# The last 512 tokens of the merge stage go as two chunks of 256 tokens, the very last chunk in two halves of 128

## The chip, the core and the metric

The kernel runs on one core of a Trainium2 chip. The metric is the device time of one execution, in microseconds (us). Three executions of the kernel before took 2415.31, 2416.16 and 2416.76 us, so its median is 2416.16 us. Engines are written as in the profile: PE is TensorE, DVE is VectorE, ACT is ScalarE, POOL is GpSimd, SP is SyncE. PE's clock has two levels, 1.2 and 2.4 GHz; the profile gives the granted clock as a share of the higher one.

## What is computed

The input x has 8 x 1024 tokens of 256 numbers. The reference, cut to what the change touches:

```python
# first half: attention and a memory MLP on the normalised tokens, merged by two gates
out_swa = _swa(x_in, wq, wk, wv, wo)
...                                   # gradients of the MLP give updated weights upd
out_mem = _mlp(*upd, k_flat)          # silu(x @ w1.T + b1) @ w2.T + b2, hidden size 1024
g1 = sigmoid(out_swa @ lin1.T)
g2 = sigmoid(out_mem @ lin2.T)
x = x + (g1 * out_swa + g2 * out_mem)
# second half: 8 experts, the top 2 of each token
h = _layernorm(x)
probs = softmax(h @ gate_w.T + gate_b)
topk_prob, topk_idx = top_k(probs, 2)
...                                   # slot of a token = its rank among the tokens of its expert
y = relu(rows @ W1[e] + b1) @ W2[e] + b2
x = x + probability * y
```

## The kernel before

The kernel has four phases, each a block of five engine programs that ends with all engines meeting: attention, gradient, merge and experts. The change is in the merge phase (about 1410 to 1945 us of the span).

**Chunks.** The merge phase takes the 8192 tokens in chunks. `SIZES` gives the blocks of 128 tokens in each; before, it is 16 chunks of 4 blocks (512 tokens), C = 0 to 15. `parts_of(C)` gives the parts in which the end of a chunk's work is done: one part of all four blocks, except for the last chunk, which has two parts of two blocks.

**Work of a chunk.** For chunk C, in fp32r products that are each split into three matmuls (`matmul_split`, L105):
- `hidden(C, t)`, t = 0 to 7: 6 matmuls each into one of three PSUM banks `ps_z`; ACT makes the sigmoid (`m_sig`, L1980), DVE multiplies (`m_hf`, L2121), ACT rounds the high half (`m_hh`, L1985), POOL subtracts to get the low half (`m_hl`, L2369; for t = 7 DVE does it, L2126). `hidden(C, t)` waits until DVE has read the bank of t - 3.
- `gate1(C)`: 12 matmuls; `memory_out(C, m, half)`: 4 times 12 matmuls, which wait for the low halves; `gate2(C)`: 12 matmuls.
- `second_term` and `merge` on DVE (L2136 and L2147), `residual`: 2 transposes for each block on PE (L1897) and an add on DVE (L2183), then the layernorm: `norm_stats` (L2191 to L2200) on DVE, the root on POOL (`root`, L2375), `norm_apply` (L2208) on DVE, transposes of the result on PE (`transpose_x2`, L1906), copy by ACT (`copy_x2T`, L2038), the router's matmuls (`router`, L1916), then on DVE the top two experts (`router`, `shift`, `choose_experts`, L2223 to L2262), exp on ACT (L2051, with a table load before it and one after it, when the next sigmoid comes), and `dispatch`: small matmuls on PE (L1928) and ten small operations on DVE (L2273 to L2292). At last POOL scatters the rows to their expert slots with indirect DMAs (L844), one for each block and each of the two choices k.

**Order.** Each engine runs a list written out by hand. In the loop's turn for chunk C the work of three chunks is interleaved: the matrix products of C, the end of C - 1 (gate2, merge, residual, norm, router) and the dispatch and scatter of C - 2. On DVE the turn is: hidden 0 and 1, `second_term(C - 1)`, hidden 2, `merge(C - 1)`, hidden 3, `weigh(C - 2)`, hidden 4, `choose_experts(C - 2)`, hidden 5 to 7, `residual(C - 1)`, the low half of hidden 7, `dispatch(C - 2)`, `norm_stats` and `norm_apply(C - 1)`, then the splits for the next chunk and the router of C - 1. On PE `transpose_x2(C - 1)` stands before the last 12 matmuls of `memory_out`, and `router(C - 1)` ends the turn. On ACT the turn ends with `copy_x2T(C - 1)`, `split_x2(C - 1)`, `memory_out(C, 1)` and `exponent(C - 1)`. In the last chunk's turn ACT and DVE also split the first expert's W1 (L2089 and L2341).

**After the loop** the last chunk's own end is done with nothing of a later chunk beside it. PE's list there:

```python
            gate2_part(NCH - 1, 0)
            dispatch(NCH - 2)
            gate2_part(NCH - 1, 1)
            keep_busy(2)
            residual(NCH - 1, 0)
            keep_busy(2)
            residual(NCH - 1, 1)
            keep_busy(12)
            ...                       # transpose_x2 and router of both parts
            keep_busy(4)
            dispatch(NCH - 1)
            keep_busy(32)
```

`keep_busy(n)` is n matmuls of 512 columns (L1956) whose results nobody reads. POOL does, after the loop, the roots of the last chunk's parts and the k = 0 scatters of the last two chunks. The k = 1 scatters of the last two chunks stand at the start of the expert phase on POOL, ahead of the gathers of its first round. The expert phase starts when all engines have ended the merge phase; SP then loads the first expert's rows once the k = 0 scatters have landed.

Of the kernel before, what the change touches and what calls it, by code (L numbers as in the profile page):

```python
# [14 lines left out]
P = 128  # L15
# [21 lines left out]
T = GRP * P  # L37
SIZES = [GRP] * (NBLK // GRP)
NCH = len(SIZES)
# [857 lines left out]
def parts_of(C):  # L897

    return [slice(0, 2), slice(2, 4)] if C == NCH - 1 else [slice(0, GRP)]

# [803 lines left out]
def merge_phase(nc, io, sems, shared, routed, halves, g1, g2, b1n, b2n, chunk_in, first_w1, first_w2):  # L1704
    with ExitStack() as ctx:
# [120 lines left out]
        def part_bank(n):  # L1826

            return ps_z[n]
# [8 lines left out]
        def tensor(e):  # L1837
# [29 lines left out]
            def gate2_part(C, n):  # L1867
                (wh, wl), cols = lin[1], columns(parts_of(C)[n])
                acc = part_bank(n)[:].rearrange("p (m t) -> p m t", m=KC)
                pe.wait_ge(*om_low.at(C, 1))  # L1870
                pe.wait_ge(*h_made.at(C, HC - 1))
                for m in range(KC):
                    mc = slice(m * P, (m + 1) * P)
                    i = matmul_split(e, acc[:, m], [(wh[:, k, mc], wl[:, k, mc]) for k in range(KC)],
                                     [(omh[:, k, cols], oml[:, k, cols]) for k in range(KC)])
                i.then_inc(*gate2_done(C, n))
# [13 lines left out]
            def residual(C, n):  # L1890
                blocks = parts_of(C)[n]
                pe.wait_ge(*merged.at(C, n))
                pe.wait_ge(*ident_in.at(0))
                pe.wait_ge(*x2T_full.at(*final_part(C - 1)))
                for j in range(blocks.start, blocks.stop):
                    for m in range(KC):
                        i = e.transpose(ps_r[:, j, m * P:(m + 1) * P], ga[:, m, j * P:(j + 1) * P], ident[:])  # L1897
                i.then_inc(*merged_T(C, n))

            def transpose_x2(C, n):  # L1900
                blocks = parts_of(C)[n]
                pe.wait_ge(*x2_made.at(C, n))
                pe.wait_ge(*x1_made.at(C, n))
                for j in range(blocks.start, blocks.stop):
                    for m in range(KC):
                        i = e.transpose(ps_r[:, j, m * P:(m + 1) * P], x2[:, j, m * P:(m + 1) * P], ident[:])  # L1906
                i.then_inc(*x2T_done(C, n))
# [66 lines left out]
        def scalar(e):  # L1974
# [17 lines left out]
            def gate2_part(C, n):  # L1992
                acc = part_bank(n)[:].rearrange("p (m t) -> p m t", m=KC)
                act.wait_ge(*merged.at(*final_part(C - 1)))
                act.wait_ge(*gate2_done.at(C, n))
                e.activation(gb[:, :, columns(parts_of(C)[n])], acc, ACTF.Sigmoid).then_inc(*gate2_made(C, n))

# [34 lines left out]
            def copy_x2T(C, n):  # L2032
                blocks = parts_of(C)[n]
                dst = x2T[:].rearrange("p m (j t) -> p m j t", t=P)[:, :, blocks]
                src = ps_r[:].rearrange("p j (m t) -> p m j t", m=KC)[:, :, blocks]
                act.wait_ge(*x2T_done.at(C, n))
# [76 lines left out]
        def vector(e):  # L2113
# [14 lines left out]
            def first_term(C):  # L2128
                dve.wait_ge(*gate1_made.at(C, 1))
                e.tensor_tensor(ga[:], ga[:], oT[C % 2][:], ALU.mult).then_inc(*term1(C))  # L2130

# [45 lines left out]
            def residual(C, n):  # L2177
# [4 lines left out]
                dve.wait_ge(*x2_made.at(*final_part(C - 2)))  # L2182
                e.tensor_tensor(x1[s][:, blocks], ps_r[:, blocks], x_t[s][:, blocks], ALU.add).then_inc(*x1_made(C, n))  # L2183

# [17 lines left out]
            def norm_apply(C, n):  # L2202
# [10 lines left out]
                dve.wait_ge(*const_set.at(3))  # L2213
                e.tensor_copy(routed.tails(C)[:, blocks, 0], tokens[:, C * GRP + blocks.start:C * GRP + blocks.stop]).then_inc(*numbered(C, n))

# [695 lines left out]
```

## Time and profile before

| what | value |
|---|---|
| median of three runs | 2416.16 us |
| the profiled execution's own time | 2417.32 us |
| its span | 2415.5 us |
| PE busy | 2356.1 us, 98% of the span |
| DVE, ACT, POOL busy | 70%, 67%, 58% |
| mean granted PE clock | 0.992 |

The span is what the profiler saw from the first to the last instruction; 1.8 us of the execution's time lie outside it. The rows below come from that execution. A timeline row gives the start, the busy time from the start of the first to the end of the last instruction of the row, the engine, the line, the operation with output and inputs, and the count; a bracket gives the idle time before it and what ended it. A window's row gives its length and then the busy time of PE, of PE's weight loads, of DVE, ACT and POOL, each with its count of instructions, then the granted clock, the DMA share and GB/s. A DMA issue's row ends with the KB of one and the us to its landing. Matmuls overlap, so the time of one in a sequence is the distance between starts, not its length.

### The profile page before, as it was taken

Reading aid. Unit: us, or ns where it says so; the run is one execution under the profiler, and the core shown is the slowest. Engines: PE = TensorE matmul, PEld = TensorE weight load, DVE = VectorE, ACT = ScalarE, POOL = GpSimd, SP = SyncE. Lnnn points to the kernel's source line nnn. Section 1 sums busy time; section 2 is a strip of 40 time slices with the busy share of each in tenths; the row PEclk is TensorE's granted clock in tenths of the full one; section 3 lists DMA queues with packets and bytes.
Section 4 is the critical chain, followed back from the end, with each engine's and each line's share of the span. In section 5 each row is a group of like instructions: output and inputs, shape, how many; then the busy total and the mean of one; then the engine's idle time right before and its main releaser. Section 6 shows DMA issues by size and latency. Waiting matters only on the chain. (4 is left out here: it accounts for less than half of the span.)

```text
span 2415.5 us, 40500 instructions
## 1 busy us (share of the span) xinstructions
PE 2356.1 (98%) x15080; PEld 2100.2 (87%) x15080; DVE 1691.2 (70%) x3644; ACT 1608.8 (67%) x2439; POOL 1401.9 (58%) x1000
## 2 busy tenths in 40 slices
PE   7999999799999999999999989999999989999998
PEld 6888888688888888888888878888888789999998
DVE  7787776466666666666666676777777757777776
ACT  4787888657777777777777556666667635555453
POOL 3565566557677666666776634666666544334433
PEclk9999999999999999999999999999999999999999
DMA  4222221533333232223332222333222045555651
GB/s 128 82 88 71 93 74 54 226 102 63 70 72 69 61 64 65 62 63 69 72 69 60 75 91 88 106 101 97 94 88 65 31 132 144 152 133 151 145 144 59
DMA packets 301540, 221.78 MB, mean 92 GB/s; under 512 B 189282, under 2 KB 270215, under 8 KB 301216
## 3 DMA queue, kind: packets, MB, share of 16 engines
q1 hardware_dynamic: 287520, 188.74, 29.1%
q0 software_dynamic: 13824, 30.44, 4.2%
q8 instruction: 120, 1.97, 0.3%
q14 instruction: 76, 0.62, 0.1%
HBM read 113.30 MB, written 72.12 MB: 77 GB/s over the span
## 5 line engine op out<-in xcount | busy, mean ns | idle before, releaser
L2640 ACT ACTIVATE e_hf<-e_ps_z,e_b 128x640 f32<-128x640 f32 x128 | 102.0, 797 | 214.7 <-PE e_ps_z L105 165.0
L2369 POOL TENSOR_TENSOR m_hl<-m_hf,m_hh 128x512 fp32r<-128x512 f32 x112 | 158.2, 1424 | 112.4 <-ACT m_hh L1985 109.8
L2767 POOL DMA_INDIRECT out<-e_ys,slot_token x80 | 83.3, 1042 | 218.9 <-DVE e_ys L2719 213.4
L105 PE MATMUL e_ps_y<-r_w_h,e_hl 128*128 128x256 f32 x640 | 180.3, 282 | 0.2 <-DVE e_ys L2719 0.2
L105 PE MATMUL e_ps_y<-r_w_l,e_hh 128*128 128x256 f32 x640 | 178.8, 279 | 0.0
L105 PE MATMUL e_ps_y<-r_w_h,e_hh 128*128 128x256 f32 x640 | 178.8, 279 | 0.0
L1569 POOL TENSOR_TENSOR halves_l<-hT_full,halves_h 128x512 fp32r<-128x512 f32 x120 | 153.7, 1303 | 38.3 <-ACT halves_h L1229 38.3
L844 POOL DMA_INDIRECT xbuf_d<-xn,scatter_rows x128 | 147.6, 1153 | 44.5 <-issue 37.8
L701 POOL TENSOR_TENSOR prob<-prob,softmax_small 128x1024 f32<-128x1024 f32 x65 | 123.3, 1897 | 70.3 <-DVE softmax_small L634 70.3
L105 PE MATMUL e_ps_z<-slotsT_h,w_l 128*128 128x320 f32 x512 | 159.5, 312 | 0.7 <-DVE slotsT_l L2697 0.7
L105 PE MATMUL e_ps_z<-slotsT_l,w_h 128*128 128x320 f32 x512 | 159.4, 311 | 0.0
L105 PE MATMUL e_ps_z<-slotsT_h,w_h 128*128 128x320 f32 x512 | 159.3, 311 | 0.0
L1427 DVE TENSOR_TENSOR new_w2T<-g_bank,new_w2T 128x512 f32<-128x512 f32 x128 | 88.5, 692 | 93.8 <-PE g_bank L105 93.8
L1223 ACT ACTIVATE hT_full<-h_wordsT 128x2048 uint16<-128x2048 uint16 x60 | 153.3, 2555 | 0.0
L105 PE MATMUL g_bank<-dpred_h,h_l 128*128 128x256 f32 x520 | 148.0, 285 | 2.9 <-DVE shared_x L1420 2.8
L105 PE MATMUL g_bank<-halves_l,keys_h 128*128 128x256 f32 (+1 forms) x528 | 147.8, 280 | 0.0
L105 PE MATMUL g_bank<-dpred_h,h_h 128*128 128x256 f32 x520 | 147.7, 284 | 0.0
L105 PE MATMUL g_bank<-dpred_l,h_h 128*128 128x256 f32 x520 | 147.7, 284 | 0.0
L105 PE MATMUL g_bank<-halves_h,keys_l 128*128 128x256 f32 (+1 forms) x528 | 147.4, 279 | 0.0
L105 PE MATMUL g_bank<-halves_h,keys_h 128*128 128x256 f32 (+1 forms) x528 | 147.3, 279 | 0.0
L1434 DVE TENSOR_TENSOR new_w1T<-g_bank,new_w1T 128x512 f32<-128x512 f32 x128 | 88.4, 691 | 83.7 <-PE g_bank L105 83.7
L1243 ACT ACTIVATE dpredT_h<-dpredT 128x512 fp32r<-128x512 f32 (+1 forms) x33 | 20.7, 627 | 182.4 <-DVE dpredT L1388 178.4
(336 smaller groups left out, 9087.6 us busy)
## 6 DMA issues: line engine op xcount, KB each, us to landing
shared_x<-in_x SPq DMA_DIRECT2D x32, 512.0 KB, 4.3
shared_xT<-xT_d SPq DMA_DIRECT2D x64, 256.0 KB, 3.6
new_w1T<-in_W SPq DMA_DIRECT2D x16, 1024.0 KB
new_w2T<-in_W SPq DMA_DIRECT2D x16, 1024.0 KB, 5.6
xbuf_d<-new_w1T SPq DMA_DIRECT2D x16, 650.0 KB
xn_d<-xn SPq DMA_DIRECT2D x32, 256.0 KB, 2.5
xT_d<-shared_xT SPq DMA_DIRECT2D x32, 256.0 KB, 2.6
oT_d<-shared_oT SPq DMA_DIRECT2D x32, 256.0 KB, 2.6
```

Of the source, the lines that this page charges most:

```text
L105: i = e.matmul(out, a, b, start=first and not onto and n == 0, stop=last and n == len(terms) - 1, skip_group_check=onto)
L701: e.tensor_tensor(p[:], p[:], sm[:, 3].unsqueeze(2).broadcast_to([P, HEADS, 2 * P]), ALU.mult).then_inc(*prob_made(g))
L844: e.indirect_dma_start(io["xbuf_d"][k], bass.IndirectOffsetOnAxis(ap=self.slot[C % 2][:, k, j:j + 1], axis=0), self.rows[C % 3][:, j], Non ...
L1223: e.activation(hT_f[b][:].bitcast(U16).rearrange("p (n s) -> p s n", s=2), wordsT[b][:].rearrange("p (s k) t -> p s (k t)", s=2), ACTF.Cop ...
L1243: e.activation(dTh[:, :, 0:N], dpf[:, :, 0:N], ACTF.Copy).then_inc(*dT_high(p))
L1427: e.tensor_tensor(dst, bank("g2", p, t)[:], dst, ALU.add).then_inc(*g2_added(p, t))
L1434: e.tensor_tensor(dst, bank("g1", p, t)[:], dst, ALU.add).then_inc(*g1_added(p, t))
L1569: e.tensor_tensor(hTl[:, ks, block[b]], hT_f[b][:, hc].rearrange("p (k t) -> p k t", k=4), hTh[:, ks, block[b]], ALU.subtract).then_inc(*m ...
L2369: e.tensor_tensor(hl[:, t, 0:N], hf[(HC * C + t) % NZ][:, 0:N], hh[:, t, 0:N], ALU.subtract).then_inc(*h_low(C, t))
L2640: e.activation(hf[(HC * i + t) % NHF][:].rearrange("p (s n) -> p s n", s=2), ps_z[t % 2][:, :, 0:HALF], ACTF.Relu, bias=b1[:, i % E, t:t + ...
L2767: e.indirect_dma_start(io["out"], bass.IndirectOffsetOnAxis(ap=token[i % 2][:, b:b + 1], axis=0), ys[:, b], None, bounds_check=NT - 1, oob ...
```

## The change

`SIZES` becomes 15 chunks of four blocks and two of two blocks, so there are 17 chunks, C = 0 to 16. The last chunk's parts are one block each. What indexed blocks by a fixed chunk size now goes by the chunk's own (`chunk_blocks`, `SIZES[C]`). In the last chunk each part's transposes go to a PSUM bank of their own (`bank_blocks`: block n goes to place 2n of `ps_r`). The orders written out by hand and the counts of `keep_busy` stay.

```diff
-SIZES = [GRP] * (NBLK // GRP)
+SIZES = [GRP] * (NBLK // GRP - 1) + [2, 2]
...
 def parts_of(C):
 
-    return [slice(0, 2), slice(2, 4)] if C == NCH - 1 else [slice(0, GRP)]
+    return [slice(0, 1), slice(1, 2)] if C == NCH - 1 else [slice(0, SIZES[C])]
+
+
+def bank_blocks(C, blocks):
+
+    return blocks if C < NCH - 1 else slice(2 * blocks.start, 2 * blocks.start + 1)
...
             def gate2_part(C, n):
                 (wh, wl), cols = lin[1], columns(parts_of(C)[n])
-                acc = part_bank(n)[:].rearrange("p (m t) -> p m t", m=KC)
+                acc = part_bank(n)[:].rearrange("p (m t) -> p m t", m=KC)[:, :, 0:cols.stop - cols.start]
...
-                        i = e.transpose(ps_r[:, j, m * P:(m + 1) * P], ga[:, m, j * P:(j + 1) * P], ident[:])
+                        i = e.transpose(ps_r[:, bank_blocks(C, slice(j, j + 1)).start, m * P:(m + 1) * P], ga[:, m, j * P:(j + 1) * P], ident[:])
...
-                        i = e.transpose(ps_r[:, j, m * P:(m + 1) * P], x2[:, j, m * P:(m + 1) * P], ident[:])
+                        i = e.transpose(ps_r[:, bank_blocks(C, slice(j, j + 1)).start, m * P:(m + 1) * P], x2[:, j, m * P:(m + 1) * P], ident[:])
...
-                e.activation(gb[:, :, columns(parts_of(C)[n])], acc, ACTF.Sigmoid).then_inc(*gate2_made(C, n))
+                e.activation(gb[:, :, cols], acc, ACTF.Sigmoid).then_inc(*gate2_made(C, n))
...
-                src = ps_r[:].rearrange("p j (m t) -> p m j t", m=KC)[:, :, blocks]
+                src = ps_r[:].rearrange("p j (m t) -> p m j t", m=KC)[:, :, bank_blocks(C, blocks)]
...
             def first_term(C):
                 dve.wait_ge(*gate1_made.at(C, 1))
-                e.tensor_tensor(ga[:], ga[:], oT[C % 2][:], ALU.mult).then_inc(*term1(C))
+                N = SIZES[C] * P
+                e.tensor_tensor(ga[:, :, 0:N], ga[:, :, 0:N], oT[C % 2][:, :, 0:N], ALU.mult).then_inc(*term1(C))
...
-                e.tensor_tensor(x1[s][:, blocks], ps_r[:, blocks], x_t[s][:, blocks], ALU.add).then_inc(*x1_made(C, n))
+                e.tensor_tensor(x1[s][:, blocks], ps_r[:, bank_blocks(C, blocks)], x_t[s][:, blocks], ALU.add).then_inc(*x1_made(C, n))
...
-                e.tensor_copy(routed.tails(C)[:, blocks, 0], tokens[:, C * GRP + blocks.start:C * GRP + blocks.stop]).then_inc(*numbered(C, n))
+                e.tensor_copy(routed.tails(C)[:, blocks, 0], tokens[:, chunk_blocks(C).start + blocks.start:chunk_blocks(C).start + blocks.stop]).then_inc(*numbered(C, n))
```

## Rows read from the trace of the kernel before

**Rows 1.** The profile's page: engines' busy time; one of its DMA issues:

```profile
PE 2356.1 (98%) x15080; PEld 2100.2 (87%) x15080; DVE 1691.2 (70%) x3644; ACT 1608.8 (67%) x2439; POOL 1401.9 (58%) x1000
...
shared_xT<-xT_d SPq DMA_DIRECT2D x64, 256.0 KB, 3.6
```

**Rows 2.** Windows, chunk 15's turn and after: length, busy time by engine, granted clock:

```profile
1885.05:1914.10 29.05, 29.05 (x156) 24.01 (x154) 22.95 (x55) 18.77 (x27) 18.17 (x14) 1.00 0.07 21
1914.10:1945.00 30.90, 23.91 (x138) 18.78 (x137) 15.78 (x86) 9.72 (x14) 12.36 (x13) 0.89 0.07 21
```

**Rows 3.** PE's timeline around the last turn and after the loop:

```profile
1885.01 0.40 PE L105 MATMUL m_ps_o<-keys_h,keys_l 128*128 128x512 f32 x1
...
1887.78 0.40 PE L105 MATMUL m_ps_z<-halves_h,w_l 128*128 128x512 f32 x1
...
1914.06 0.38 PE L105 MATMUL m_ps_z<-keys_h,keys_l 128*128 128x256 f32 x1
...
1923.89 4.60 PE L1956 MATMUL m_ps_z<-keys_h 128*128 128x512 f32 x12
1928.33 1.28 PE L1906 MATMUL m_ps_r<-r_ident,xn_full 128*128 128x128 f32 x8
...
1933.96 9.15 PE L1956 MATMUL m_ps_z<-keys_h 128*128 128x512 f32 x32
1944.97 2.08 PE L2585 MATMUL e_ps_z<-w_h 128*128 128x512 f32 x8 [1.86 <-PEq L2446]
```

**Rows 4.** DVE's timeline in the last turn (chunk 15) and after the loop:

```profile
1888.61 1.23 DVE L2136 TENSOR_TENSOR gate<-gate,memT 128x1024 f32<-128x1024 f32 x1 [1.43 <-ACT gate L2002]
...
1890.76 2.27 DVE L2147 TENSOR_TENSOR gate<-gate 128x1024 f32<-128x1024 f32 x1
...
1895.80 1.34 DVE L2262 TENSOR_TENSOR router_hot<-expert_ids,router_idf 128x32 bf16<-128x32 f32 x2
...
1907.57 0.15 DVE L2214 COPY xn<-token_numbers 128x4 f32<-128x4 f32 x1
...
1909.43 2.35 DVE L2341 TENSOR_TENSOR w_l<-new_w1T,w_h 128x1024 fp32r<-128x1024 f32 x2
1913.25 0.75 DVE L2155 SCALAR_TENSOR_TENSOR keys_l<-m_ps_o,new_b,keys_h 128x512 fp32r<-128x512 f32 x1 [1.48 <-ACT keys_h L2012]
...
1918.75 0.29 DVE L2273 TENSOR_TENSOR router_pos_e<-m_ps_s,expert_counts 128x32 f32<-128x32 f32 x2 [2.04 <-remote]
...
1933.25 0.29 DVE L2262 TENSOR_TENSOR router_hot<-expert_ids,router_idf 128x32 bf16<-128x32 f32 x2
```

**Rows 5.** ACT's timeline, the end of chunk 14's turn and the start of 15's:

```profile
1877.87 1.03 ACT L2038 ACTIVATE xn2T<-m_ps_r 128x1024 f32<-128x1024 f32 x1 [1.45 <-PE m_ps_r L1906]
...
1885.05 1.27 ACT L1980 ACTIVATE m_sig<-m_ps_z,new_b 128x512 f32<-128x512 f32 x2
```

**Rows 6.** Groups by line and shape, DVE: count, busy us, mean ns of one:

```profile
L2121 DVE SCALAR_TENSOR_TENSOR m_hf<-m_ps_z,new_b,m_sig 128x512 f32<-128x512 f32 x128 | 92.7, 742 | 54.1 <-ACT m_sig L1980 51.7 <-issue 2.3
...
L2140 DVE SCALAR_TENSOR_TENSOR gate<-m_ps_o,new_b,gate 128x256 f32<-128x256 f32 x4 | 1.7, 476 | 0.0
L2147 DVE TENSOR_TENSOR gate<-gate 128x512 f32<-128x512 f32 x2 | 1.4, 692 | 0.1
```

**Rows 7.** The chain that ended last, one of its longest pieces: 256-column matmuls:

```profile
2366.34 14.27 PE e_ps_y L105 x120
```

**Rows 8.** POOL's timeline: scatters of chunk 13, first and last; last k = 0 scatter; last first-round gather:

```profile
1906.39 1.16 POOL L844 DMA_INDIRECT xbuf_d<-xn,scatter_rows  x1 [0.20 <-issue]
...
1916.77 0.98 POOL L844 DMA_INDIRECT xbuf_d<-xn,scatter_rows  x1 [0.30 <-issue]
...
1941.51 0.98 POOL L844 DMA_INDIRECT xbuf_d<-xn,scatter_rows  x1 [0.30 <-issue]
...
1963.88 1.45 POOL L2760 DMA_INDIRECT token_rows<-out,slot_token  x1 [0.30 <-issue]
```

**Rows 9.** DVE's timeline, its first use of a gathered row in the expert phase:

```profile
1973.54 0.48 DVE L2712 SCALAR_TENSOR_TENSOR token_rows<-e_b,slot_prob,token_rows 128x256 f32<-128x256 f32 x1
```

More of the change, by code:

```diff
@@ L1992, in gate2_part @@
             def gate2_part(C, n):
-                acc = part_bank(n)[:].rearrange("p (m t) -> p m t", m=KC)
+                cols = columns(parts_of(C)[n])
+                acc = part_bank(n)[:].rearrange("p (m t) -> p m t", m=KC)[:, :, 0:cols.stop - cols.start]
                 act.wait_ge(*merged.at(*final_part(C - 1)))
                 act.wait_ge(*gate2_done.at(C, n))
-                e.activation(gb[:, :, columns(parts_of(C)[n])], acc, ACTF.Sigmoid).then_inc(*gate2_made(C, n))
+                e.activation(gb[:, :, cols], acc, ACTF.Sigmoid).then_inc(*gate2_made(C, n))
             def gate2(C):
```

## The prediction

> **What bounds the kernel now.** The page comes first: PE is busy for 98% of the span, DVE for 70% [rows 1]. That is an average over four phases, so the question is who sets the time at the end of the merge phase, the only place where chunks change. Chunk 15's turn is 31.9 us on PE: from 1882.2 (twelve matmuls ahead of the row at 1885.01) to 1914.06 [rows 3]. The windows show that PE never rests in it, and that DVE works 22.95 of 29.05 us [rows 2]. After it come 30.9 us in which PE is "busy" for 23.9, but most of that is filler; here a chain of small steps decides. PE's timeline gives the marks: gate2 of the last chunk at 1914.06, the last norm's transposes at 1928.33, the last filler at 1933.96, and the first instruction of the expert phase at 1944.97 [rows 3]. That last one waited 1.86 us behind the end of the filler (1943.11); POOL's last scatter had ended at 1942.49 [rows 8]. So the end of the merge phase is the start of the 32 filler matmuls plus 11.0 us, and POOL is 0.6 us behind being the bound. The expert phase after it is PE's and does not change in shape.
>
> So the sum is over one stretch: from the moment at which ACT is free for the sigmoids of chunk 15, 1885.05 [rows 5], to 1944.97. Before: 59.9 us.
>
> **What PE's own work says.** A 512-column matmul costs (1887.78 - 1885.01) / 12 = 0.231 us [rows 3], a 256-column one 14.27 / 120 = 0.119 [rows 7]. Two short ones cost 0.007 more than a long one; over the 120 matmuls of a chunk that is 0.8 us. If PE stayed the bound, the split would be nearly free. What doesn't shrink is elsewhere.
>
> **Turn of chunk 15, now short (A).** Its own products are halved, but beside them stand the end of chunk 14 and the dispatch of 13, both of full size. PE's work: hidden 48 x 0.119, gate2(14) 2.77, gate1 1.43, memory_out 5.7, transposes of 14 about 1.6, dispatch 0.4, router 1.7: 19.3 us. DVE's list, in its written order, up to the end of `norm_apply(14)`: in the full turn it took from 1885.05 to 1907.57, 22.5 us [rows 4, 5]. From it I take: eight `m_hf` at 742 less 476 ns [rows 6], 2.1; the low half of hidden 7, 0.3; the gate2 result comes earlier, because PE has two short hiddens in front of it, and of the 1.43 us idle ahead of `second_term` [rows 4] 1.0 goes; and two contentions ease. `merge` took 2.27 us at 1024 elements, where `second_term` of the same size took 1.23, and the two `router_hot` took 1.34 in the loop and 0.29 after it, where POOL stands still [rows 4]. Their excess is 1.04 and 1.05. POOL's subtractions become about half as long, so I let half of both go, 1.0 (bounds: nothing goes, or all 2.1). A is 22.5 - 4.4 = 18.1 us to x2 of chunk 14.
>
> The Trainium skill (SBUF — State Buffer, section "Who interferes with whom") says that of a GpSimd op and a two-input VectorE op on SBUF the second to issue waits until the first has ended. By that alone the merge would pay at most one shortened POOL operation; it moves the sum inside the bounds already given.
>
> Then PE transposes (1.0 with the wait), and ACT's list: before, from `copy_x2T` at 1877.87 to the next sigmoid at 1885.05 took 7.2 us, with a table load, exp and a table load in it [rows 5]. Only `memory_out(15, 1)` in it is shorter, 0.5. So ACT is ready for chunk 16 after 18.1 + 1.0 + 6.7 = 25.8 us. A full turn took 31.9, half of one would be 16.
>
> On SP's queue the load of oT for chunk 16 waits for `merge(14)`, some 6 us into A; 256 KB land in about 4 us [rows 1] and ACT rounds them only after `memory_out(15, 0)`, some 15 us into A. This is hidden, with 5 us to spare.
>
> **Turn of chunk 16, short (B).** Now the end of chunk 15 is half-sized too. DVE's 22.5 us less 2.4 (m_hf and hidden 7), 0.5 (`second_term` to 0.69), 1.6 (`merge` to 0.69 [rows 6]), 0.5 (`residual`), 1.5 (statistics and apply, two blocks instead of four), 0.3 (root), 1.2 (idle ahead of gate2's result and sigmoids), 0.5 (half of the excess of `router_hot`): 14.0 us to x2 of chunk 15. Chunk 14's full dispatch is still in it. PE's work in this turn is 16.4 us by the same prices. POOL is behind with chunk 13's eight scatters, 11.4 us from first to last [rows 8]; they would start some 17 us into A and end about 2.5 us into B, after which the first `m_hl` of chunk 16 follow; they are needed only by `memory_out`, so this is hidden.
>
> Then DVE goes on in order: low half of memory_out 0, first term, W1's split of the first expert (2.35 [rows 4], unchanged), low half of memory_out 1: 0.4 + 0.7 + 2.35 + 0.45, 3.9 us. Before, from 1907.6 to 1914.0, it was 6.4, with 1.48 idle [rows 4].
>
> **After the loop (C).** Before: from 1914.0 to 1944.97, 31.0 us. Routing of two blocks instead of four, and less wait ahead of the dispatch at 1918.75 [rows 4]: 1.3 less. Second term, merge, residual and norm at one block a part would be 3.4 less on DVE, but the twelve fillers stand between the last residual transposes and the last norm's transposes. They took 4.44 us (1923.89 to 1928.33 [rows 3]), while DVE's share from merge to apply shrinks below that. So filler that was just hidden becomes the path, and of these 3.4 us only 1.6 are gained (bound: 2.6 if the fillers run at 9.15 / 32 = 0.286 us each, as the last 32 do). The norm's transposes, copy, router matmuls and choice of two blocks: 5.2 us (1928.33 to 1933.5) become 3.5, 1.7 less. The 32 fillers and the 1.86 us wait behind them stay: 11.4. So C is 31.0 - 4.6 = 26.4 us. POOL's last scatter batch falls from four to two, about 2.6 us less, which gains nothing, because PE's filler ends later than POOL; without that cover it would be worth 0.6 at most. POOL must also finish chunk 14's eight scatters ahead of the last two roots: 11.4 us against some 12 that the chain leaves; it is next in line if DVE gets quicker.
>
> The expert phase begins with four k = 1 scatters instead of eight, 5.1 us less on POOL. But the last first-round gather was issued at 1963.88 and DVE first used a row at 1973.54 [rows 8, 9], so this was hidden: nothing.
>
> **Sum.** 25.8 + 14.0 + 3.9 + 26.4 = 70.1 us, against 59.9: 10.1 us slower. The profiled execution took 2417.3 (span 2415.5), so 2427.4; the median is 1.2 us lower, 2416.2, so I take 2416.2 + 10 = 2426.2.
>
> **Rivals.**
> *1. The turns stay at PE's pace; not slower.* DVE and ACT are not full in any window [rows 2], and smaller pieces let each start earlier. The place is the two short turns; they would cost 19.3 + 16.4 = 35.7 us from 1882.2 against 31.9 before, 3.8 more, and C gives back 4.6: 2415.4, no change. It decides where the stalls of A and B together stay under about 5 us. The Trainium skill (Perfetto Trace Analysis, section "Optimizing Scalar/DVE Operations") says that where these engines aren't saturated but cause bubbles on others, breaking up instructions may let work finish sooner; this would be that case, with about that result. Against it: DVE's own list of A is 18.1 us before the transposes may start, in order, and the ACT list behind it can't start before; both are sums of single operations. *2. PE's clock falls.* In A and B PE would be idle a quarter to a third of the time, and after the loop it is slower already (0.89 in the last window [rows 2]). At 1.2 GHz a 256-column matmul is about twice 0.119. Over half of both turns this makes PE's work 19.3 x 1.5 = 29 and 16.4 x 1.5 = 24.6 us, against 25.8 and 17.9 by the chains above: 10 us more, 2436. Against it: most of the gaps are short ones between bursts. *3. The order makes DVE and ACT wait for each other more.* A hidden step is only 6 x 0.119 = 0.71 us of PE, and `merge` and `choose_experts` hold up `m_hf`, behind which ACT's next sigmoid waits. My subtraction keeps only the waits of before; if contention stays whole (1.5 us) and each turn gets another 2 us, it is 2431.5.
>
> **Chances.** Forecast (slower by 6 to 13 us) 0.70; rival 1 0.14; rival 2 0.07; rival 3 0.09. The bounds: contention -1.5 to +1.5, filler -1, in-order waits up to +3, the first-order subtractions some 2 us either way; this gives 2421.5 to 2430.5 for the likeliest alone. To hold 8 in 10 I go into rivals 1 and 3: 2420 to 2432. A change under 0.2%, 4.8 us, can't be told from none here. Slower by more 0.84, within 0.14, faster 0.02 (rival 1 with full-speed filler and a still shorter start of the expert phase).
>
> **What would show it.** The first `m_sig` of chunk 16 about 26 us after that of chunk 15 (right), or 19 (rival 1). PE idle ahead of `transpose_x2` of chunks 14 and 15 with DVE's apply as releaser, 3 us and 1 to 2 us. `merge` of chunk 14 under 2.27 us. The twelve fillers running straight into the last L1906 transposes while DVE's last apply has ended over 1 us before. 32 fillers, then 1.86 us, then the expert phase, at about 1955. From there to the end 470.5 us, as before. The prediction is wrong if PE has no gaps in the short turns, if the granted clock is 0.5 inside them, or if the expert phase changes its length.

## The result, and the profile after

The changed kernel took 2426.12 us (median of 7 runs, 2422.75 to 2427.11), the kernel before beside it 2416.53 us (7 runs, 2415.17 to 2418.88). The ratio is 1.0037, 95% interval [1.0025, 1.0049]: slower by 9.6 us, as forecast (2426.2). The profiled execution took 2424.82 us.

The page: span and busy times, with 116 more recorded matmuls for the extra chunk.

```profile
span 2423.0 us, 40845 instructions
...
PE 2360.4 (97%) x15196; PEld 2108.8 (87%) x15196; DVE 1693.3 (70%) x3682; ACT 1615.6 (67%) x2470; POOL 1402.4 (58%) x1008
```

The span grew by 7.5 us. The first sigmoid of chunk 15 starts 0.75 us later than before (1885.80 against 1885.05 [rows 5]); from there to the start of the expert phase it is 66.57 us instead of 59.92; the expert phase takes 470.6 us instead of 470.5. So 6.65 of the 7.5 us lie in the stretch that the prediction summed. The 0.75 us ahead of it is no effect of the change: in the twelve traces that have the split at the end or not at all, the first sigmoid of chunk 15 lies between 1885.04 and 1890.03, in both kernels alike. ACT's timeline gives both marks of the short turn, and what it waits for ahead of the second:

```profile
1885.80 0.84 ACT L1985 ACTIVATE m_sig<-m_ps_z,new_b 128x256 f32<-128x256 f32 x2
...
1904.44 1.02 ACT L2044 ACTIVATE xn2T<-m_ps_r 128x1024 f32<-128x1024 f32 x1 [3.96 <-PE m_ps_r L1911]
...
1911.08 0.24 ACT L2057 ACTIVATE router_probs<-logits_below 128x40 f32<-128x40 f32 x1 [1.78 <-DVE logits_below L2242]
...
1912.62 0.84 ACT L1985 ACTIVATE m_sig<-m_ps_z,new_b 128x256 f32<-128x256 f32 x2
```

Turn A took 26.8 us. In the windows (turn A, two slices in it, turn B, after it, expert phase) PE is no longer full as it was in [rows 2], and its clock falls to 0.50, the 1.2 GHz level:

```profile
1885.80:1912.60 26.80, 22.68 (x161) 21.72 (x160) 17.38 (x62) 15.98 (x31) 16.55 (x17) 0.85 0.15 44
1904.00:1906.00 2.00, 2.00 (x13) 2.00 (x12) 1.46 (x3) 1.56 (x2) 1.70 (x2) 0.59 0.04 11
1906.00:1908.00 2.00, 2.00 (x12) 2.00 (x11) 0.00 (x0) 1.99 (x3) 1.39 (x3) 0.50 0.04 11
1912.60:1927.70 15.10, 13.87 (x116) 13.22 (x114) 11.26 (x43) 9.23 (x24) 6.80 (x10) 0.93 0.06 19
1927.70:1952.40 24.70, 21.26 (x127) 16.92 (x127) 15.09 (x75) 11.40 (x18) 13.69 (x14) 1.00 0.06 16
1952.40:2423.00 470.60, 460.27 (x3474) 457.46 (x3474) 333.92 (x561) 231.56 (x254) 183.57 (x165) 0.99 0.51 136
```

DVE's timeline, against [rows 4]: `merge` and `router_hot` are shorter, the cast between them is longer (0.71 us, before 0.30), and DVE waits for the root on POOL.

```profile
1889.79 1.35 DVE L2154 TENSOR_TENSOR gate<-gate 128x1024 f32<-128x1024 f32 x1
...
1893.03 0.71 DVE L2263 CAST router_idf<-router_idx 128x8 f32<-128x8 uint32 x1
1893.77 0.29 DVE L2269 TENSOR_TENSOR router_hot<-expert_ids,router_idf 128x32 bf16<-128x32 f32 x2
...
1901.83 1.43 DVE L2215 TENSOR_SCALAR xn_full<-x,m_mv,m_rstd 128x256 f32<-128x256 f32 x4 [1.16 <-POOL m_rstd L2382]
1903.18 0.15 DVE L2221 COPY xn<-token_numbers 128x4 f32<-128x4 f32 x1
...
1927.70 0.16 DVE L2221 COPY xn<-token_numbers 128x2 f32<-128x2 f32 x1
...
1931.04 0.48 DVE L2162 SCALAR_TENSOR_TENSOR keys_l<-m_ps_o,new_b,keys_h 128x256 fp32r<-128x256 f32 x1
...
1933.32 0.25 DVE L2280 TENSOR_TENSOR router_pos_e<-m_ps_s,expert_counts 128x16 f32<-128x16 f32 x2
...
1940.30 0.41 DVE L2215 TENSOR_SCALAR xn_full<-x,m_mv,m_rstd 128x256 f32<-128x256 f32 x1 [0.83 <-POOL m_rstd L2382]
```

The wait of 1.16 us for the root is not new. Chunk 15's turn in the kernel before has the same one:

```profile
1906.23 1.42 DVE L2208 TENSOR_SCALAR xn_full<-x,m_mv,m_rstd 128x256 f32<-128x256 f32 x4 [1.16 <-POOL m_rstd L2375]
```

PE's timeline, against [rows 3]: the wait for DVE, the router at the low clock, and the two fillers (the second row shows 31 of the last 32). The row at 1940.76 waits for DVE (0.47 us), not for the twelve fillers ahead of it.

```profile
1903.31 1.09 PE L1911 MATMUL m_ps_r<-r_ident,xn_full 128*128 128x128 f32 x8 [2.80 <-DVE xn_full L2215]
...
1906.69 3.42 PE L1921 MATMUL m_ps_s<-gate_w,xn2T 128*128 128x8 f32 x16
...
1927.84 0.66 PE L1911 MATMUL m_ps_r<-r_ident,xn_full 128*128 128x128 f32 x4 [0.49 <-DVE xn_full L2215]
...
1937.31 2.98 PE L1961 MATMUL m_ps_z<-keys_h 128*128 128x512 f32 x12
1940.76 0.95 PE L1911 MATMUL m_ps_r<-r_ident,xn_full 128*128 128x128 f32 x4 [0.47 <-DVE xn_full L2215]
...
1944.71 7.23 PE L1961 MATMUL m_ps_z<-keys_h 128*128 128x512 f32 x31
1952.37 2.06 PE L2592 MATMUL e_ps_z<-w_h 128*128 128x512 f32 x8 [0.44 <-PEq L2453]
```

POOL's timeline: chunk 14's eight scatters (first, last), the last two roots right behind them, and chunk 16's last scatter.

```profile
1927.21 1.16 POOL L844 DMA_INDIRECT xbuf_d<-xn,scatter_rows  x1 [0.20 <-issue]
...
1938.67 0.98 POOL L844 DMA_INDIRECT xbuf_d<-xn,scatter_rows  x1 [0.30 <-issue]
1939.66 1.11 POOL L2382 TENSOR_TENSOR m_rstd<-m_rstd,m_neg_half 128x1 f32<-128x1 f32 x2
...
1948.74 0.97 POOL L844 DMA_INDIRECT xbuf_d<-xn,scatter_rows  x1 [0.30 <-issue]
```

The reader is to see two things in the last two fences. POOL went from its last scatter of chunk 14 into the roots without idle, and DVE's last `norm_apply` waited for them. And POOL's last scatter ends at 1949.71, 2.66 us before the expert phase; before, that distance was 2.48 us (1942.49 to 1944.97 [rows 3, 8]).

### The profile page after: what moved, and what is told of

Read it like the earlier page. It is cut to its first block and busy times, and to the rows that moved or that the text cites. A ratio compares the mean times of both kernels' runs of the same rounds, so it can differ in the third digit from the quotient of the medians.

```text
span 2423.0 us, 40845 instructions
## 1 busy us (share of the span) xinstructions
PE 2360.4 (97%) x15196; PEld 2108.8 (87%) x15196; DVE 1693.3 (70%) x3682; ACT 1615.6 (67%) x2470; POOL 1402.4 (58%) x1008
## 5 line engine op out<-in xcount | busy, mean ns | idle before, releaser
L2376 POOL TENSOR_TENSOR m_hl<-m_hf,m_hh 128x512 fp32r<-128x512 f32 (+1 forms) x119 | 159.7, 1354 | 116.0 <-ACT m_hh L1990 114.6
```

What stands on the lines that cost most here:

```text
L2376: e.tensor_tensor(hl[:, t, 0:N], hf[(HC * C + t) % NZ][:, 0:N], hh[:, t, 0:N], ALU.subtract).then_inc(*h_low(C, t))
```

## The experiments

Two theories of the stretch stood. **T1**: in the short turns the in-order lists of DVE and ACT set the pace. **P**: after the loop POOL's scatters set the end, not the filler as the prediction had it. Rivals: PE's clock, ACT's table loads, the two halves of the last chunk. "Stretch" is the time from the first sigmoid of chunk 15 to the start of the expert phase in the profiled execution.

**The changed kernel once more.**

> The changed kernel itself again, beside the others, as their reference. Expected: 8 to 10 us over the kernel before, with the first short turn (first m_sig of chunk 15 to first m_sig of chunk 16) at 26 to 27 us, and the expert phase starting 2.5 to 2.7 us after POOL's last scatter.

Measured: 2425.34 us, ratio 1.0037 [1.0023, 1.0052]. Turn A 25.8 (just under the 26 to 27 expected), turn B 13.7, stretch 65.2 us. Here the clock stayed higher in turn A (0.93) and fell after the loop. The windows of turn A and of seven us after the loop:

```profile
1890.00:1915.80 25.80, 21.68 (x172) 20.70 (x171) 17.38 (x62) 16.01 (x32) 15.69 (x16) 0.93 0.15 45
1936.00:1943.00 7.00, 6.91 (x22) 5.13 (x22) 5.71 (x22) 2.28 (x3) 5.59 (x8) 0.52 0.15 45
```

In this slow piece lie the twelve fillers. They took 4.45 us instead of 2.98, and the last norm's transposes followed them with no wait, 0.7 us after DVE's last apply had ended (1943.16 with its copy):

```profile
1939.57 4.45 PE L1961 MATMUL m_ps_z<-keys_h 128*128 128x512 f32 x12
1943.86 0.60 PE L1911 MATMUL m_ps_r<-r_ident,xn_full 128*128 128x128 f32 x4
```

So one kernel has its low-clock stretch in different places in different executions, and a difference of 1 us in one turn of one trace says nothing of the edit. The kernel before varies as much: its stretch is 59.9 us in the profile of before, and in the two versions below that only shorten its last filler 59.7 and 57.7.

**The split in the middle of the merge phase.** The kernel before, with two short chunks in place of its eighth, and its last chunk as it was. Blocks are indexed by the chunk's own size, as in the change.

```diff
-SIZES = [GRP] * (NBLK // GRP)
+SIZES = [GRP] * 7 + [2, 2] + [GRP] * 8
...
-    return [slice(0, 2), slice(2, 4)] if C == NCH - 1 else [slice(0, GRP)]
+    return [slice(0, 2), slice(2, 4)] if C == NCH - 1 else [slice(0, SIZES[C])]
```

> The two short chunks stand in the middle (chunks 7 and 8 of 17) and the last chunk is again one of 512 tokens in two halves, so nothing at the end of the merge phase is shortened. Theory T1 (a short turn costs about as much as a full one on DVE and ACT, because the neighbours' work in it stays full-sized): first short turn 25 to 27 us, second 19 to 21, the full turn behind it 30 to 32, together 75 to 79 instead of 63.7 for two full turns: 11 to 15 us over the kernel before. Rival 1 (PE's pace): 1 to 2 us over.

Measured: 2431.9 us, 1.0062 [1.0045, 1.0079], 15.4 us above its before (2416.51). ACT's timeline, the first sigmoids of both short chunks and of the third full one behind them (those of the first and second full one start at 1678.42 and 1712.46):

```profile
1632.86 0.84 ACT L1985 ACTIVATE m_sig<-m_ps_z,new_b 128x256 f32<-128x256 f32 x2
...
1658.77 0.84 ACT L1985 ACTIVATE m_sig<-m_ps_z,new_b 128x256 f32<-128x256 f32 x2
...
1743.58 1.27 ACT L1985 ACTIVATE m_sig<-m_ps_z,new_b 128x512 f32<-128x512 f32 x2
```

The turns are 25.9, 19.7, 34.0 and 31.1 us, 110.7 together, where three turns of 31.87 are 95.6: 15.1 us more, which is the whole difference. 13.7 of it are the two short turns (45.6 against 31.87), 2.2 the full one behind them, -0.8 the last. The time and the full turn behind came out above the expectation (15.4 against 11 to 15 us, 34.0 against 30 to 32). At the end of the phase the full turn behind is missing and the work after the loop gives something back. The first short turn came out at the predicted A (25.8).

**DVE's dispatch moved into the wait for the root**, in the two short turns only.

```diff
-                if sent:
+                if sent and C < NCH - 2:
                     dispatch(C - 2)
...
                     norm_stats(C - 1, 0)
+                    if C >= NCH - 2:
+                        dispatch(C - 2)
```

> The changed kernel; in the turns of the two short chunks DVE does dispatch(C - 2) between norm_stats and norm_apply of C - 1, so that it works while POOL takes the root (1.16 and 0.84 us idle), instead of before norm_stats. Theory T1 (DVE's list in order sets when transpose_x2 may start in the short turns): x2 of chunk 14 is done 1.2 us earlier after the first m_sig of chunk 15 (16.2 instead of 17.4 us), that of chunk 15 0.8 earlier; each turn is shorter by about as much; in all 1 to 2 us quicker. Theory T2 (PE's own work at the lower clock sets the short turns): x2 is earlier, but the turns keep their length.

Measured: 2426.4 us, 1.0033 [1.0021, 1.0044]; stretch 66.5. DVE's timeline shows the wait of 1.16 us gone:

```profile
1900.84 0.17 DVE L2207 TENSOR_SCALAR m_rstd<-m_mv 128x4 f32<-128x4 f32 x1
1900.92 0.28 DVE L2280 TENSOR_TENSOR router_pos_e<-m_ps_s,expert_counts 128x32 f32<-128x32 f32 x2
...
1902.40 1.38 DVE L2215 TENSOR_SCALAR xn_full<-x,m_mv,m_rstd 128x256 f32<-128x256 f32 x4
1903.69 0.17 DVE L2221 COPY xn<-token_numbers 128x4 f32<-128x4 f32 x1
```

From the sigmoid to this copy it is 16.3 us instead of 17.4. Turn A is 23.95 us, and 23.75 in the run with both edits, against 25.0 to 26.8 in the six traces whose turn A has DVE's list as it was. So T1 holds for turn A: DVE's list shortens it by at least what is taken from it. In turn B no gain is seen: 14.4 and 14.7 us, against 15.1 and 13.7 in the two looks at the changed kernel. The stretch and the time stay the same too (1 to 2 us were expected), because x2 of chunk 15 to the expert phase grew from 24.7 to 28.2 us. Of these 3.5 us, 0.8 is the filler: POOL's last scatter ended at 1950.48, the filler at 1953.61, 0.30 before the phase, so now the filler was the later one. The other 2.7 us arose ahead of POOL's last scatter, in a piece with PE's clock at 0.68 (1935 to 1940) and with a wait of 2.04 us on DVE whose releaser the trace does not name. Whether the edit caused these was not tested.

**A shorter last filler**, 20 matmuls instead of 32, in the changed kernel and in the one before, and 24 in the one before.

```diff
-            keep_busy(32)
+            keep_busy(20)
```

> The changed kernel with the last 32 filler matmuls cut to 20. In the changed kernel the fillers ended 7.8 us after the last choice of experts, POOL's last scatter 5.5 us after it, and the expert phase started 8.2 us after it. Theory P (POOL's last scatter sets the end of the merge phase, the fillers are covered): still 8.2 us, no change of time. Theory F (the fillers set it, as the prediction said): about 6.0 to 6.5 us, 2 us quicker, unless PE's clock is at its lower level for longer at the start of the expert phase, which would give back up to 2 us.

> The kernel before with the last 32 fillers cut to 20. Before, fillers ended 9.6 us after the last choice of experts, POOL's last scatter 9.0 us, the expert phase started 11.4 us after it. Theory P: still 11.4 us and the same time. Theory F: 10.8 us, 0.6 quicker. If POOL's end is followed by the expert phase after the same 2.5 us in this kernel and in the changed one, P holds in both, and the prediction was wrong to count nothing for the two scatters fewer.

> The kernel before with 24 instead of 32 matmuls in the last filler. Theory P: in the kernel before POOL's last scatter ended 0.6 us ahead of the filler; with 20 matmuls the expert phase started 2.50 us behind POOL and the execution was at 0.9992 of before. With 24 the filler ends some 1 us ahead of POOL's last scatter, the start stays 2.5 us behind POOL, 59.7 us from the first m_sig of chunk 15; 0.9990 to 1.0000. Rival: the filler's end was the bound as predicted, and 8 matmuls at 0.231 to 0.286 us give 1.9 to 2.3 us, 0.6 of them ahead of POOL and the rest nowhere: the same number, so this run tells only whether some full version is faster than before by over 0.2% (not expected).

Measured: changed with 20, 2424.59 us, 1.0019 [1.0009, 1.0029]; before with 20, 2417.95 us, 0.9992 [0.9983, 1.0002] (its before 2419.84); before with 24, 2416.84 us, 1.0000 [0.9991, 1.0010] (its before 2416.89). The timelines of the kernel before with 20, PE and then POOL's last scatter:

```profile
1938.39 6.61 PE L1956 MATMUL m_ps_z<-keys_h 128*128 128x512 f32 x20
1949.27 1.19 PE L2585 MATMUL e_ps_z<-w_h 128*128 128x512 f32 x2 [4.27 <-PEq L2446]
```

```profile
1945.80 0.97 POOL L844 DMA_INDIRECT xbuf_d<-xn,scatter_rows  x1 [0.30 <-issue]
```

The wait behind the filler grew from 1.86 us [rows 3] to 4.27, the distance to POOL's last scatter stayed: 2.50. In the changed kernel with 20 the filler ended at 1950.90 and POOL's last scatter at 1951.32; the phase started at 1953.98, 2.66 behind POOL, and the stretch was 66.1. So the filler was not the bound; the start follows POOL's last scatter in both kernels. With 24 matmuls before it is 2.49 (1944.80 to 1947.29); the stretch there was 57.7 us, not the 59.7 expected. In the changed kernel the filler was only just hidden: 0.43 us lay between its end and the phase, and in no trace was it less than 0.30.

The times moved more than the start of the phase did. The changed kernel with 20 lies 1.8 us below the two other changed versions timed beside it (2426.4 and 2426.54), and the kernel before with 20 lies 1.9 us below its before, which is within its interval. The traces point the same way. PE's transposes of the first expert's rows wait for those rows to be loaded. In the four traces with 20 matmuls in the last filler they start 5.2 to 6.1 us behind POOL's last scatter, in the nine others 6.5 to 8.0. The part from the start of the expert phase to the end takes 468.7 to 469.5 us in the four, and 469.9 to 471.7 in the others, except for 467.2 in one. So a shorter filler may be worth 1 to 2 us behind the mark at which the stretch ends. Why was not tested.

**Two of the last four scatters left out**, in the kernel before, with 20 matmuls in the last filler. This leaves out the first-choice rows of the last 256 tokens.

```diff
-        for j in range(SIZES[C]):
+        for j in range(2 if (k, C) == (0, NCH - 1) else SIZES[C]):
```

> The kernel before with 20 last fillers instead of 32, and with the k = 0 scatters of the last 256 tokens left out (two of the last four; their rows are not computed by the experts). Theory P (POOL's last scatter sets the end of the merge phase): the expert phase starts 8.8 us after the last choice of experts instead of 11.4, 2.6 us earlier, still 2.5 us behind POOL's last scatter. Theory F (PE's fillers): it starts as in the run with 20 fillers alone, 11.3 us after it.

Measured: 2412.92 us, 0.9985 [0.9975, 0.9994] (its before 2416.51): 3.6 us faster. POOL's last scatter and PE's start of the expert phase:

```profile
1940.75 0.97 POOL L844 DMA_INDIRECT xbuf_d<-xn,scatter_rows  x1 [0.30 <-issue]
```

```profile
1936.56 6.02 PE L1956 MATMUL m_ps_z<-keys_h 128*128 128x512 f32 x20
1944.08 2.09 PE L2585 MATMUL e_ps_z<-w_h 128*128 128x512 f32 x8 [1.49 <-PEq L2446]
```

From the end of the last `router_hot` (1936.11) to the phase it is 8.0 us (8.8 expected); in the kernel before it was 11.4 (1933.54 to 1944.97), 11.3 with 20 matmuls and all scatters, and 10.7 with 24. So two scatters are worth 2.7 to 3.4 us there. Two starts at 1.28 us make 2.56 of it; the rest is the time to the first of the last scatters, 3.4 us here and with 24 matmuls, 4.0 with 20, without an edit to it. In the changed kernel, which has two scatters fewer by its own shape, the distance is 8.2. P is shown for the start of the phase. In the time, this run lies 3.6 us below the kernel before, and the one with 20 matmuls and all scatters 1.9 below, so by the times the two scatters alone are worth some 1.7 us, less than the intervals can tell.

**PE filled while it waits**: ten matmuls ahead of `transpose_x2(14)`.

```diff
+                if C == NCH - 2:
+                    keep_busy(10)
```

> The changed kernel with 10 filler matmuls (2.3 us) on PE in the 2.8 us gap ahead of transpose_x2(14) in the first short turn. Theory C (that gap lets PE's clock fall to 1.2 GHz from 1904 to 1913 us, and the router's matmuls at 3.4 instead of 1.9 us and the last memory_out at 2.4 instead of 1.4 lengthen ACT's wait for exp): the granted clock stays at 1.0 in this turn, the first turn goes from 26.8 to about 25 us, the second loses up to 1 us, in all 2 to 3 us quicker. Theory T1 alone: the clock is a side effect and nothing changes by more than 0.5 us.

Measured: 2426.54 us, 1.0029 [1.0018, 1.0041]. The windows of turn A and of eight us after the loop:

```profile
1886.50:1912.30 25.80, 23.32 (x188) 21.74 (x187) 17.30 (x62) 16.16 (x33) 15.16 (x16) 1.00 0.16 45
1932.00:1940.00 8.00, 8.00 (x36) 6.63 (x35) 5.74 (x27) 3.69 (x6) 5.93 (x7) 0.57 0.04 8
```

The clock stayed at 2.4 GHz through turn A, and the turn took 25.7 us, as in the second look at the changed kernel; x2 of chunk 14 was done 0.7 us later than there (18.05 us after the first sigmoid). The clock fell after the loop, and the stretch was 66.5. The second look shows the same fall without the ten matmuls, so it is not shown that filling the gap moved it. No time was gained, where 2 to 3 us were expected if the clock set the turn. And in the run with both edits, below, the clock was 0.99 to 1.00 in each piece of the stretch, which still took 63.2 us. So the clock is a part of the spread and not the cause of the 9.6 us.

**No table loads in the turn**: exp replaced by the sigmoid in the router's probabilities, so the probabilities are other numbers.

```diff
-                e.activation(pr[:, 0:SIZES[C]], below[:, 0:SIZES[C]], ACTF.Exp).then_inc(*exp_made(C))
+                e.activation(pr[:, 0:SIZES[C]], below[:, 0:SIZES[C]], ACTF.Sigmoid).then_inc(*exp_made(C))
```

> The changed kernel with exp replaced by the sigmoid in the router's probabilities (this changes what is computed there), so that ACT loads no table between the turns: 1.28 us twice for each chunk. Theory T1: in full turns PE hides this and nothing changes; in the first short turn ACT's list is on the path, and the turn is 1.3 to 2.6 us shorter, the total 1.3 to 3 us. If PE or DVE alone set the short turns, nothing changes.

Measured: 2425.51 us, 1.0036 [1.0023, 1.0048]; no gain against 2425.34 of the changed kernel on the same chip. T1's number (1.3 to 3 us quicker) missed; what had been expected if ACT's loads are off the path, no change, came true. Turn A took 26.7 us. ACT's timeline:

```profile
1907.90 0.48 ACT L2018 ACTIVATE keys_h<-m_ps_o,new_b 128x256 fp32r<-128x256 f32 x1
1911.24 0.24 ACT L2057 ACTIVATE router_probs<-logits_below 128x40 f32<-128x40 f32 x1 [2.86 <-DVE logits_below L2242]
1911.78 0.47 ACT L1985 ACTIVATE m_sig<-m_ps_z,new_b 128x256 f32<-128x256 f32 x1 [0.31 <-PE m_ps_z L105]
```

The load ahead of exp had only filled ACT's wait for the logits; without it the wait is 2.86 us instead of 1.78. The load behind exp gained 1.0 us at most, and then PE's first product came 0.31 us late and the next 0.81. In this execution, again at a low clock (0.65 from 1903 to 1910), the path ran through DVE's apply, PE's transposes, memory_out and router, and DVE's logits.

**The last chunk in one part** of two blocks instead of two halves.

```diff
-    return [slice(0, 1), slice(1, 2)] if C == NCH - 1 else [slice(0, SIZES[C])]
+    return [slice(0, SIZES[C])]
...
             gate2_part(NCH - 1, 0)
             dispatch(NCH - 2)
-            gate2_part(NCH - 1, 1)
             keep_busy(2)
             residual(NCH - 1, 0)
-            keep_busy(2)
-            residual(NCH - 1, 1)
             keep_busy(12)
```

> The changed kernel, but the last chunk's end goes in one part of two blocks instead of two halves of one block; the fillers stay at 2 + 12, the second 2 go. Theory P (in the changed kernel POOL's eight scatters of chunk 14 end at 1939.66, no idle before the last roots, so the halves have nothing to gain ahead of the root): from x2 of chunk 15 (1927.70 in the profile after) to the last router_hot it takes 16.5 us there; with one part the merge, add and statistics of 256 columns end before POOL is free, and only the steps behind the root (apply, transposes, copy, router) are done without overlap, about 0.5 to 1 us; with the root of both blocks as one operation 0.3 us less. So within 1 us of the changed kernel, 2424.5 to 2427, ratio to before 1.0035. Rival: the halves overlap all of DVE's, PE's and ACT's steps and are worth as much as the second part's chain, 3 us; then 2428 to 2430.

Measured: 2424.86 us, 1.0029 [1.0019, 1.0038], as expected by P. From x2 of chunk 15 to the end of the last `router_hot` it took 17.7 us instead of 16.5. But the second look at the changed kernel has 17.65 there (1929.51 to 1947.16), so a gain by the halves is not shown, in the traces or in the times. Its roots, too, stood right behind chunk 14's last scatter. In this trace the clock stayed at 1.00 through both turns, which are those of the changed kernel; B took 14.0 us, and A, as this window shows, 25.0:

```profile
1888.81:1913.84 25.03, 20.93 (x178) 19.96 (x177) 17.28 (x62) 15.98 (x31) 15.09 (x16) 1.00 0.16 47
```

**Both edits**: DVE's dispatch in the root's wait, and 20 matmuls in the last filler.

> The changed kernel with both edits that the runs so far speak for: in the two short turns the dispatch of C-2 stands between norm_stats and norm_apply of C-1 on DVE, and the last filler has 20 matmuls instead of 32. The first alone shortened turns A and B by 2.5 us together, but the expert phase then began 3.43 us behind POOL's last scatter, since the 32 fillers ended at 1953.61 and had become the later of the two. Theory P: with 20 fillers (3.4 us less) POOL's last scatter sets the end again, the expert phase starts 2.65 us behind it, and of the 2.5 us some 1 us comes through (POOL's list behind chunk 14's scatters takes the rest); 2423 to 2424.5, ratio 1.0010 to 1.0025, first m_sig of chunk 15 to expert start 65 us. Rival: nothing adds up, since POOL's eight scatters of chunk 14 set the place of the last roots whatever DVE does; then as with 20 fillers alone, 1.0019, 66.1 us.

Measured: 2420.76 us (its before 2416.89, the one part version beside it 2424.86); ratio 1.0019 [1.0010, 1.0029]. The stretch was 63.2 us, better than either theory's number. POOL's timeline, the end of chunk 14's scatters, the roots, and the last scatter:

```profile
1937.22 0.97 POOL L844 DMA_INDIRECT xbuf_d<-xn,scatter_rows  x1 [0.30 <-issue]
1938.20 1.11 POOL L2384 TENSOR_TENSOR m_rstd<-m_rstd,m_neg_half 128x1 f32<-128x1 f32 x2
...
1947.31 0.97 POOL L844 DMA_INDIRECT xbuf_d<-xn,scatter_rows  x1 [0.31 <-issue]
```

The phase started at 1950.93, 2.65 behind POOL. POOL's eight scatters began 38.7 us after the first sigmoid of chunk 15 (1926.49 less 1887.76), where in the changed kernel it was 41.4 in the first look and 39.0 in the second. The gain in the turns came through in this trace, with the shorter filler and with the clock at 0.99 to 1.00 all through the stretch; which of the two let it through, one trace does not tell. By the ratio it is no better than the shorter filler alone, though; the two were not timed side by side. No version with the two short chunks came down to the kernel before, and of the full versions of the kernel before none is faster by more than its interval.

## Why the prediction was right

The sign held, and so did the mechanism of the two short turns. That the time fits to 0.1 us (2426.2 against 2426.12) is luck: inside the sum one term was 5.5 us too large, the stretch grew by 6.65 us and not by 10.1, and 3 us from outside it made up for the rest.

| step | predicted | changed kernel | the same once more |
|---|---|---|---|
| DVE to x2 of chunk 14 | 18.1 | 17.4 | 17.4 |
| turn A | 25.8 | 26.8 | 25.8 |
| turn B | 14.0 (to x2) | 15.1 | 13.7 |
| to the end of the low half of memory_out 1 | 3.9 | 3.8 | 3.8 |
| after the loop (C) | 26.4 | 20.9 | 21.9 |
| whole stretch | 70.1 | 66.6 | 65.2 |
| expert phase | 470.5 | 470.6 | 470.1 |

**Turns A and B: right.** 39.8 us predicted; 41.9, and 39.5 in the second look. PE waited 2.80 us for DVE's apply in A (3 predicted) and 0.49 in B (1 to 2 predicted, too much). In the trace of the one part version, with the clock at 1.00, A is 25.0 us (17.4, 1.3 and 6.4, where 18.1, 1.0 and 6.7 were predicted). Contention eased by more than the half that was assumed: `merge` 1.35 us from 2.27, `router_hot` 0.29 from 1.34, though the cast ahead of it took 0.71 from 0.30; that is 1.6 us, not 1.0. Against it, the idle time ahead of `second_term` fell by 0.4 us only (1.07 from 1.43, 1.0 predicted). The split in mid-phase repeats A at 25.9 us, and moving DVE's dispatch shortens it. The Trainium skill (SBUF — State Buffer, section "Who interferes with whom") lets the second of such a pair wait for the first; the trace agrees. An undisturbed subtraction takes 0.74 us here. The one that began 0.82 us before `merge` (1888.97) had nearly ended, and `merge` paid 0.12 over `second_term`'s 1.23; the one that began inside `merge` (1890.40) took 1.33. The second to come paid each time: `merge` 0.12 us, POOL 0.59. The idle of 1.16 us for the root is in the 22.5 us that the working started from, so it was not missing.

**Rival 1 (PE's pace) fell**: the first sigmoids are 26.8 us apart, not 19. The rule of the Trainium skill cited for it (Perfetto Trace Analysis, section "Optimizing Scalar/DVE Operations") says only that it may help, and it does not give the result here: the pieces were broken up, but the end of a full chunk and the dispatch of another stand beside a short one in each engine's order.

**Rival 2 (the clock) is true in part.** The clock fell to 0.50 inside turn A, so one of the prediction's own signs of being wrong ("if the granted clock is 0.5 inside them") came true for 2 of 26.8 us. It cost 1 us there against the second look and 1.8 against the trace with the clock at 1.00 (the 16 router matmuls took 3.42 us, there 1.85). It did not last over both turns, PE was idle for 15% of A and 8% of B and not for a quarter to a third, and the 10 us that it was priced at did not come.

**Rival 3 (more in-order waits)** did not come ahead of x2 of chunk 14, which DVE reached after 17.4 us and not 18.1. One new wait stands behind it: ACT waited 1.78 us for DVE's logits ahead of exp in A, 0.74 in the second look and not at all with the clock at 1.00.

**C: the term that was mis-sized, 26.4 against 20.9 us.** The prediction took 4.6 us off the old 31.0; 10.1 went. These are the parts, from the first profile of each kernel:

| part of C | before | after | gained | predicted |
|---|---|---|---|---|
| low half of memory_out 1 to the dispatch | 4.75 | 1.80 | 2.95 | 1.3 |
| dispatch to the last norm's transposes | 9.58 | 7.44 | 2.14 | 1.6 |
| transposes to the end of the last `router_hot` | 5.21 | 3.43 | 1.78 | 1.7 |
| from there to the expert phase | 11.43 | 8.18 | 3.25 | 0 |

- "less wait ahead of the dispatch": I took 1.3 us for dispatch and routing together. The dispatch began 0.4 us after the end of `router_hot`, where before the wait ahead of it alone was 2.04 us [rows 4].
- "filler that was just hidden becomes the path": in the first profile it did not. The twelve ran in 2.98 us, not 4.44, at a clock of 1.00, and the apply behind them waited for POOL's root, with chunk 14's scatters ahead of the last roots; this is what the prediction called "next in line". In the second look they ran in 4.45 us and were the path, by 0.7 us. So this sentence holds or not with the place of the clock's fall.
- "which gains nothing, because PE's filler ends later than POOL": this was wrong, and it is the largest part. The expert phase followed POOL's last scatter by 2.36 to 2.66 us in eleven of thirteen traces (2.48 before, 2.66 after), whatever the filler did. It followed by more in two, by 3.4 (DVE's dispatch moved) and 4.2 us (the last chunk in one part), and in both the filler's end lay only 0.30 us ahead of the phase. I had read the filler's 1.86 us wait as its own fixed cost. It was the rest of POOL's. Of the 3.25 us, 2.56 are the two scatters fewer; the dispatch of two blocks instead of four ahead of them gave 0.85, and the phase started 0.2 us later behind the last scatter than before.

**Why the total still fit.** The stretch grew by 6.65 us in the traces, not 10.1. The profiled execution of before lies 0.8 us above its median of the later runs (2417.32 against 2416.53), that of after 1.3 us below (2424.82 against 2426.12), and 0.75 us arose before the stretch: 6.65 + 0.75 + 0.1 + 0.8 + 1.3 = 9.6. In the second look the profiled execution is 1.8 us above its median, with a stretch of 65.2. So part of the 9.6 us, 3 to 4, is not in the stretch of any one trace. What it is stays open. One trace does not show the median: the start of chunk 15 varies by 5 us among the twelve, the stretch of the kernel before by 2.2, and the expert phase by 4.6 among all thirteen.

**The halves of 128 tokens and the four k = 1 scatters fewer in the expert phase** gave nothing that shows: 2424.86 us in one part, and 470.6 us against 470.5.

## What to carry to other kernels

Splitting a step of a hand-ordered pipeline shortens only its own work; in each turn the neighbours' work, still of full size, stays in every engine's list, so price the turn as the longest in-order chain and not as half a turn of the fullest engine (25.0 to 26.8 and 13.7 to 15.1 us here, where half a turn was 16). At the end of a phase, measure the distance from each engine's last instruction to the next phase's start in more than one version; the one that stays constant is the bound, and a wait behind a filler may belong to another engine. Look also at the first instruction of the next phase that does real work: with the shorter filler it moved where the start of the phase did not. When a few tenths of a microsecond separate two engines, a cut on the one makes the other the path, as the filler was when DVE's dispatch moved. And take more than one profile of a version before you credit 1 or 2 us of it to an edit.

## What the runs showed of the hardware

- The fall of PE's clock to 1.2 GHz moved between executions of the same kernel: mostly in turn A in one (0.50 from 1906 to 1908), after the loop in the other (0.52 from 1936 to 1943). In the trace in which one gap of PE was filled it was 1.00 there and fell after the loop (0.57 from 1932 to 1940); that the filling did this is not shown.
- With POOL's subtractions at 256 columns, the 1024-element add on DVE took 1.35 us instead of 2.27. But a cast of 8 elements a partition took 0.71 us in the loop (1893.03 to 1893.74), over the same time as a POOL subtraction (1892.97 to 1893.71), and ended with it. In the kernel before it took 0.30 in the loop and again ended with a subtraction (1800.16 after 1800.14); where none ran it took 0.17 (1915.71). So even the smallest operation seems to be held until the subtraction ends; this was not tested by itself.
- Indirect DMAs on POOL follow each other at 1.28 us (1938.67 after 1937.40), and where PE's filler had ended in time, the next phase started 2.36 to 2.66 us behind the end of the last one.
